# Issuing the products of probabilities and values for two units at once in every second slot

## The reference, cut to what matters

```python
x = x + L0_xattn(layernorm(x), ctx, ...)   # 8 heads of 8, tokens along the last axis, banded
x = x + L0_ffn(layernorm(x), ...)          # top half of the tokens, gelu, scattered back
x = x + L1_xattn(layernorm(x), ctx, ...)   # 32 query heads of 8, 8 key/value groups
x = x + L1_ffn(layernorm(x), ...)          # relu squared, an expert matrix scaled by top-2 logits
```

```python
# L0: 256 tokens, a band of +-64; q, k, v from one projection of x
attn = softmax(where(band, q @ k.T / sqrt(8), min))
o = einsum('bhqk,bkhd->bqhd', attn, v)
# L1: 64 queries and 64 keys of a sample, keys and values from the context
attn = softmax(q @ k.T / sqrt(8))
out = einsum('bhqk,bhkd->bhqd', attn, v)
```

## Time and profile before

| | |
|---|---|
| median of the timed runs | 378.01 us |
| span of the profiled execution, first to last instruction | 376.2 us |
| TensorE busy | 348.0 us (92%) |
| VectorE busy | 256.4 us (68%) |
| ScalarE busy | 209.9 us (56%) |
| GpSimd busy | 193.1 us (51%) |

### The profile page before, as it was taken

The page is one execution under the profiler, slowest core; times in us unless marked ns, Lnnn a source line. Parts: engine busy times, 40 slices in busy tenths (PEclk is TensorE's granted clock), DMA queues, the critical chain, the costliest instruction groups (busy, mean ns, idle before and its releaser), DMA issues.

```text
span 376.2 us, 7398 instructions
## 1 busy us (share of the span) xinstructions
PE 348.0 (92%) x2258; PEld 261.4 (69%) x2258; DVE 256.4 (68%) x935; ACT 209.9 (56%) x438; POOL 193.1 (51%) x287
## 2 busy tenths in 40 slices
PE   0689999989899999999999899899999999999993
PEld 0577767666676666666668688676776767888892
DVE  5899788998989989877223615664567855662264
ACT  2648787758677686866642241466556874312310
POOL 4648868747857675855520251413233363233833
PEclk9959999999999999999999999999999999999999
DMA  7995000000000000000000000000000000000001
GB/s 217 350 375 192 3 0 3 1 2 3 1 2 0 3 3 1 3 2 1 3 2 0 0 2 0 1 2 0 2 1 2 2 0 3 0 16 28 1 30 42
DMA packets 10150, 12.16 MB, mean 32 GB/s; under 512 B 1920, under 2 KB 8832, under 8 KB 10112
## 3 DMA queue, kind: packets, MB, share of 16 engines
q1 hardware_dynamic: 9536, 11.36, 8.7%
q10 hardware_dynamic: 576, 0.33, 0.3%
HBM read 10.64 MB, written 1.05 MB: 31 GB/s over the span
## 4 chain that ended last, share of the span: by engine, by line
PE 72%; DVE 17%; issue 4%; ACT 3%; POOL 2%; DMA 1%; POOLq 0%; SPq 0%; DVEq 0%; ACTq 0%
PE O L377 10%; PE S L339 7%; PE S L666 6%; PE ST L361 6%; DVE masked L1110 4%; PE S L472 4%; PE ST L690 4%; PE O L623 3%; PE PJ L310 3%; PE S L536 2%; PE S L608 2%; PE PJ L449 2%; PE PJ L579 2%; PE XB L391 2%; PE PJ L311 2%
## 5 line engine op out<-in xcount | busy, mean ns | idle before, releaser
L1110 DVE CUSTOM_DVE_ANT_0 masked<-S,band 128x192 bf16<-128x192 f32 x256 | 79.9, 353 | 17.0 <-PE S L339 15.0
L785 ACT ACTIVATE ex<-ST 128x384 f32<-128x384 f32 x128 | 62.5, 490 | 17.7 <-PE ST L361 16.2
L948 POOL TENSOR_SCALAR rstd<-mv 128x1 f32<-128x1 f32 x40 | 11.8, 294 | 98.3 <-DVE mv L1074 98.3
L377 PE MATMUL O<-ex,v 128*32 128x192 f32 x512 | 58.5, 338 | 0.0
L339 PE MATMUL S<-qk 128*128 128x384 f32 x128 | 54.0, 427 | 3.3 <-DVE mw L1110 1.7
L361 PE MATMUL ST<-qk 128*128 128x192 f32 x256 | 48.9, 273 | 0.0
L960 POOL TENSOR_TENSOR qk<-kp,kmask 128x1024 fp32r<-128x1024 f32 x24 | 45.7, 1909 | 4.6 <-DVE kp L1208 4.6
L361 PEld LDWEIGHTS ST<-qk 128*128 128x128 f32 x256 | 45.2, 191 | 1.7 <-issue 1.2
L339 PEld LDWEIGHTS S<-qk 128*128 128x128 f32 x128 | 25.0, 197 | 17.2 <-issue 12.8
L751 ACT ACTIVATE hs<-PJ,sb,cols 128x512 fp32r<-128x512 f32 x29 | 22.5, 777 | 25.5 <-PE PJ L311 25.3
L1254 DVE TENSOR_REDUCE mw<-S 128x8 f32<-128x512 f32 x32 | 22.0, 687 | 19.3 <-PE S L536 19.1
(11 more groups left out here) (178 smaller groups left out, 774.8 us busy)
## 6 DMA issues: line engine op xcount, KB each, us to landing
w<-in_w SPq DMA_DIRECT2D x2, 1024.0 KB, 10.0
cx<-in_cx SPq DMA_DIRECT2D x1, 1024.0 KB, 8.1
cxT<-in_cxT SPq DMA_DIRECT2D x1, 1024.0 KB, 9.6
up<-in_up SPq DMA_DIRECT2D x1, 1024.0 KB, 10.8
down<-in_down SPq DMA_DIRECT2D x1, 1024.0 KB, 11.9
out<-x SPq DMA_DIRECT2D x8, 128.0 KB, 1.7
x<-in_x SPq DMA_DIRECT2D x1, 768.0 KB, 6.7
vecs<-in_vecs SPq DMA_DIRECT2D x1, 640.0 KB, 8.4
```

What stands on the lines that cost most here:

```text
L377: last = mm(O[32 * j:32 * j + 32, T * g + BAND * c:T * g + BAND * c + WIN], v0[:, t % 2, c, b, 4 * g + j, :], ex[:, (n // 2) % 4, j, :], s ...
L785: A(ex[:, (n // 2) % 4, 2 * w:2 * w + 2, :], ST[n % 2][:, 0:2 * WIN].rearrange("p (h k) -> p h k", h=2), ACT.Exp, scale=SCALE).then_inc(s[ ...
L1110: last = V.tensor_tensor_reduce(out=masked[:, n % 2, h, :], in0=S[n % 2][:, WIN * h:WIN * h + WIN], in1=band[:, c, :], scale=1.0, scalar=N ...
```

## The change

Both loops issue the products of two units in every odd slot and none in the even ones. In the first attention the units l-1 and l of the tile before come in slot l = 1, 3, 5, ... 15; in the second, units n-7 and n-6 in every odd n. So an even unit's product comes one slot later than its lag says, except where it already did (unit 0 of eight, unit 0 of four); odd units keep their slot. The waits in the loop's body and all other engines' programs are as they were.

```diff
-                for t, r in {0: (), 1: (place(T_, l, PV_LAG + 1), place(T_, l, PV_LAG))}.get(l % 8, (place(T_, l, PV_LAG),)):
+                for t, r in ((place(T_, l, PV_LAG + 1), place(T_, l, PV_LAG)) if l % 2 else ()):
                     if not live(t, r):
                         continue
                     n = UNITS * t + r
...
-                for u in {2: (), 3: (n - 7, n - 6)}.get(n % 4, (n - 6,)):
+                for u in ((n - 7, n - 6) if n % 2 else ()):
                     if not 0 <= u < 4 * TILES:
                         continue
                     t, l = divmod(u, 4)
```

## The result

The changed kernel takes 362.12 us (median of four runs, 362.10 to 362.44), the kernel before, timed beside it, 377.96 us (377.83 to 378.04): a ratio of 0.958, with a 95% interval of 0.9567 to 0.9594. That is 15.8 us less; 19 were forecast. The profiled execution has a span of 360.4 us, against 376.2.

A forecast was written before the change was run, and what follows sets the result against it. TensorE was taken as the bound, with VectorE 7% behind; 8.4 + 1.5 + 6.0 + 4.0 = 19.9 us, taken as 19, gave a 357.2 us span and 359.0 us median, forecast range 353.5 to 364 us (0.66).

The forecast's parts named there:

- The price of a block on TensorE: Both attentions: a pair costs what a single unit costs; each block removed saves 0.54 us, about 0.6 in the second.
- The edit moves only even units, and none is late: Both attentions: even units come one slot later, what waits for products waits for odd ones; nothing counted for late units.
- Second attention: Eight blocks fewer: 2.4 us from the first four places, 1.6 from the last four, together 4.0 us (ends 2.5 and 5.0).
- VectorE takes over in steps 1 to 6: First six tile steps: VectorE becomes the bound, so 8.4 us of its waits plus 1.5 us of its work go.
- 9.9 - 1.5 = 8.4 us go: Tile steps 1 to 6: of VectorE's 9.9 us waiting for scores, 1.5 stay in the selection loop.
- I credit half of it: Tile steps 3 to 6: half of L1156's 1.0 us stretch beside GpSimd's L960 goes in three of four, 1.5 us.
- VectorE keeps waiting for scores though TensorE idles: Sign that the prediction is wrong; VectorE's waits for scores were to fall from 9.9 to about 1.5 us.
- Step 7: Tile steps 7 and 8: VectorE has time to spare, so 6.0 us go together, about 2.8 of it in step 7.
- That collision is already there and cannot come twice: Argument against the rival that VectorE is stretched further beside GpSimd's L960 (368 us, chance 0.18): L960 starts only after VectorE's kp.
- the ends of -4 and +4 us: Bounds on the 1.5 us VectorE credit: L1156's stretch all gone, or another two-input instruction falling under L960 instead.
- The clock: Rival: TensorE's waits drop its clock to 1.2 GHz; 403 us if steps 3 to 6 ran so, chance 0.03.
- From span to median: Whole kernel: the median of timed runs lies 1.8 us above the profiled span, added to 357.2 us.

The follow-up runs named there:

- e7: Changed kernel, but first-attention pairs made of two units sharing their column groups, as many double blocks: 373.6 us, measured once.
- e2: Kernel before with the new pairing in the second attention only, the first attention as before: 374.05 us.
- e5: Changed kernel with VectorE's L1156 and L1159 (token scores) moved from slot 0 to slot 1: 359.96 us.
- e8: Changed kernel with GpSimd's third key instruction in slot 13 instead of 14, L1151 from slot 15 to 0, L1156 from 0 to 1: 357.11 us.
- e3: Changed kernel with GpSimd's third key instruction writing 8 of 256 columns from tile 2 on, leaving out part of the keys: 357.02 us.
- e9: Kernel before, single blocks kept, with GpSimd's third key instruction in slot 13, L1151 in slot 0, L1156 in slot 1: 375.70 us.
- e6: Changed kernel with first-attention products (L377) over 16 of 192 columns from the second tile on: 365.85 us.
- e4: Changed kernel with the third projection of the next tile in slot 10 instead of 9: 366.10 us.
- e10: Changed kernel with the product pair of slots 1 and 9 issued in slots 2 and 10, behind the scores of unit 10: 364.35 us.
- e11: As e10, the pair of slots 1 and 9 issued in slots 2 and 10, but on the reordered kernel of e8: 357.85 us.

## Why the prediction was right, and where it was short

**The price of a block on TensorE: right.** 0.54 us each were counted; step 8, where nothing but TensorE bounds, gives 3.37 / 6 = 0.56. e7 shows that the four column groups carry it.

**The edit moves only even units, and none is late: right as far as the traces show.** Step 8 is filled by TensorE as before, and no wait for `ex` or the values appears.

**Second attention: right, the exact figure partly by luck.** 4.0 us (e2), with L591 starting within 0.1 us of the end of `on` in tiles 3 to 5, as worked out. But the first four places gave 2.8 us instead of 2.4 (from the first L623 to L591 of tile 2, 33.54 us before and 30.69 after) and the last four 1.2 instead of 1.6 (from there to L591 of tile 6, 28.73 and 27.55).

**VectorE takes over in steps 1 to 6: right in kind, 3.0 us too large.** 9.9 us were forecast and 6.9 came. By the step's own terms: VectorE's waits for scores fell by 4.8 us instead of 8.4. Of the 3.6 us too many that stay, steps 1 and 2 hold 1.6 (0.5 and 1.1 us, where the sum left none), steps 3 to 5 some 1.3 (two waits of 0.4 us each instead of one) and step 6 0.8. The rest of VectorE's idle time, 3.1 us (13.0 - 9.9), which the sum left alone, fell to 2.3. VectorE's busy time fell by 1.3 us, near the 1.5 credited, but by luck and not for my reason: L1156 gave nothing in steps 4 to 6 (it gave 0.9 in step 3, because L1151 was under L960 ahead of it), and L1151 took 1.45 us more at the turn to step 3 and L1191 1.3 in all; what made up for these were small pieces, the closer sequence of the L1110 above all (1.5 us), then L1208 (0.6) and the L1151 of step 6, which now falls behind the end of the window (0.4). Two steps failed. The larger is "9.9 - 1.5 = 8.4 us go": 4.8 went, and what holds the rest stays open. The other is "I credit half of it": L1156 was to start nearer to the end of L960, but the shorter steps moved GpSimd's third instruction along with VectorE. e5 shows that the credit was real, 0.54 us in each of three steps; it needed an edit of its own. The prediction named as a sign of being wrong that "VectorE keeps waiting for scores though TensorE idles"; that came in part, 5.1 us of waits while TensorE was idle for 14.3 of 121.5 us.

**Step 7: 1.3 us short.** The second collision of L1151, 1.33 us longer than its usual 0.41, stands at its beginning (152.22 us) and accounts for that much. In e8, without it, step 7 takes 15.88 us, 2.6 less than before, against about 2.8 forecast.

**"That collision is already there and cannot come twice": wrong.** I had looked at GpSimd's keys in slot 5 only. The collision that came is in slots 14 and 15, with an instruction that read one tensor in SBUF and that I had therefore left out. The trace of the kernel before had the warning: L1169, a `tensor_scalar` with one tensor in SBUF, took 0.93 to 1.16 us in steps 3 to 6, where it runs beside the L960 of slot 5, and 0.35 in the other four tiles.

```profile
L1169 DVE TENSOR_SCALAR sel<-slot,rk x8: 345/637/1161, 79.9 to 212.8; 128x128 f32<-128x128 f32 x8
```

The price of the collision that came lies inside the ends of -4 and +4 us, on the other side from the value taken. e3 and e8 show that it costs the changed kernel about 5 us, and e8 with e9 that 2.8 us of this came with the change: in the new order it brings 18.6 us. That this stands so near to the 19 is again partly luck, for in that order too the waits for scores fell by 5.9 us and not by 8.4.

The Trainium skill ("SBUF — State Buffer", Who interferes with whom) names this case too, beside the rule that the prediction used: copies and `tensor_scalar` in a mode that uses both ports take the pair shared with GpSimd. The trace agrees: L1151 and L1077 are `tensor_scalar` on float32 in SBUF, and take 1.67 to 2.15 us where they lie under L960, against about 0.41.

**The clock: no fall in the changed kernel, as forecast; two variants had one.** TensorE waits 13 us in steps 1 to 6 and stays at 2.4 GHz. In e3 it fell for 3.4 us at 138.9 us, after TensorE had been busy 1.84 of 3.40 us with one wait of 1.65, and in e6 for 17 us.

**From span to median:** 1.7 us, as the 1.8 assumed.

**Open.** What sets the second wait of steps 3 to 5 wasn't isolated: e4, e10 and e11 only moved it. Why L1077 meets L960 in step 2 in some orders and not in others follows from hundredths of a microsecond that I can't forecast; where the edge lies, the last section says. And e6's question, what TensorE's blocks are still worth in steps 3 to 6, has no answer free of the clock and of VectorE's new collisions.

## What to carry to other kernels

When an engine's load is cut and a second engine becomes the bound, its busy time from the profile is not a floor given by nature: here instructions of that engine which lay beside a third engine's long ones were stretched, and each shortening shifted which ones met. Before such an edit, list the long instructions of GpSimd and every VectorE instruction within a slot of them, those with one input too, and place them apart in the same edit; here that was worth 8.0 us beside the 15.8. Here a second unit on column groups of its own cost 0.01 us (0.46 against 0.45), and one on the same groups 0.3 us (0.77).

## What the runs showed of the hardware that was not expected

- Who is stretched when L960 meets VectorE's L1151 or L1077 turns on a few hundredths of a microsecond. In all fourteen traces, every one of these that started behind L960, or up to 0.10 us ahead of it, ended 0.15 us after it: L1077 in e8 started at 58.45 us, L960 at 58.54, and the one took 2.13 us, the other its usual 1.90. Those that started 0.12 to 0.26 us ahead of it kept their length, and L960 was the longer, by 0.14 us at most: 2.03 us behind one 0.12 us ahead (e5), 1.93 behind one 0.25 us ahead, 1.89 alone. The changed kernel, in step 2, is just on the good side:

```profile
59.30 0.41 DVE L1077 TENSOR_SCALAR xn<-x,mv,rstd 128x256 f32<-128x256 f32 x1
```

```profile
59.44 2.01 POOL L960 TENSOR_TENSOR qk<-kp,kmask 128x1024 fp32r<-128x1024 f32 x1
```

- VectorE's L1156 takes 0.42 us alone, 0.94 (e5) or 1.48 when it starts inside L960, and 1.94 almost under the whole of it (e4); it ended 0.3 us after L960 each time. L960 took 2.33 us once, where VectorE's copy L1148 had started 0.20 us ahead of it (65.86 against 66.06 us) and ran to 66.64.
- With TensorE's own work shortened (e6), its granted clock fell from 2.4 to 1.2 GHz three times, with no wait longer than 1.31 us in the 3.4 us ahead of the fall at 94.4 us.
